# 18 pairs of the first head's maxima between the projections of chunks 11 to 15, and VectorE's rotation steps behind GpSimd's sine

## The reference

```
x:  4 x 2048 x 256, 16 heads of 16
qkv = x @ w_qkv + b_qkv
q, k: from token 679 on, x * cos + rotate_half(x) * sin   (1369 rows of sin and cos)
attn = softmax(q k^T / 4);  out = attn v;  y = out @ w_proj + b_proj
x = layernorm(x + y)
gate, up = fp4(x) @ fp4(w_gate)^T, fp4(x) @ fp4(w_up)^T      (704 wide, blocks of 16)
x = layernorm(x + fp4(silu(gate) * up) @ fp4(w_down)^T)
```

## Time and profile before

| | us |
|---|---|
| median of 3 runs | 3471.18 (3470.55 to 3475.24) |
| profiled execution, its own time | 3468.84 |
| its span, first to last instruction | 3466.9 |
| TensorE busy in it | 3373.9 (97%) |
| VectorE | 3219.7 (93%) |
| ScalarE | 2652.9 (77%) |
| GpSimd | 811.9 (23%) |
| mean granted TensorE clock | 0.983 |

### The profile page before, as it was taken

How to read it: one execution, slowest core, us unless ns; L and a number is a source line. 1 busy time by engine, 2 the same in 40 slices (tenths; PEclk the granted TensorE clock), 3 DMA queues, 4 the chain that set the end, 5 groups by cost and what they waited for, 6 DMA issues and landing times.

```text
span 3466.9 us, 69292 instructions
## 1 busy us (share of the span) xinstructions
PE 3373.9 (97%) x27752; PEld 1516.5 (44%) x27752; DVE 3219.7 (93%) x3525; ACT 2652.9 (77%) x4946; POOL 811.9 (23%) x1045
## 2 busy tenths in 40 slices
PE   8989999999999999999999999999999999999998
PEld 4543333333333333333333333333333346677775
DVE  6778999999999999999999999999999949999997
ACT  5626888888888888888888888888888874444444
POOL 5830210101111001101010110011000016766665
PEclk9978999999999999999999999999999999999999
DMA  4531222222222122211122221122111112211110
GB/s 147 180 121 63 103 91 85 95 84 104 73 85 77 66 79 104 73 55 70 64 82 82 85 89 54 61 83 78 62 61 67 50 40 66 78 50 42 42 36 22
DMA packets 132973, 264.19 MB, mean 76 GB/s; under 512 B 30022, under 2 KB 84518, under 8 KB 114214
## 3 DMA queue, kind: packets, MB, share of 16 engines
q1 hardware_dynamic: 119520, 243.25, 19.9%
q10 hardware_dynamic: 13132, 16.52, 1.5%
HBM read 173.11 MB, written 84.93 MB: 74 GB/s over the span
## 4 chain that ended last, share of the span: by engine, by line
PE 83%; DVE 6%; ACT 4%; POOL 3%; issue 2%; DMA 1%; SPq 0%; ACTq 0%; POOLq 0%; DVEq 0%
PE ps L677 37%; PE ps L730 33%; PE ps L814 6%; PE ps L826 3%; ACT arena L941 2%; PE ps L740 1%; PE ps L717 1%; PE ps L648 1%; ACT arena L916 1%; POOL arena L1273 1%; PE ps L804 1%; DVE arena L1082 1%; POOL arena L1282 0%; DVE arena L1166 0%; DMA arena<-in_xT 0%
## 5 line engine op out<-in xcount | busy, mean ns | idle before, releaser
L1082 DVE TENSOR_REDUCE arena<-ps 128x1 f32<-128x1024 f32 x2048 | 2495.3, 1222 | 61.0 <-PE ps L677 44.9
L941 ACT ACTIVATE arena<-ps 128x512 f32<-128x512 f32 x4096 | 2222.0, 597 | 321.5 <-PE ps L717 236.5
L677 PE MATMUL ps<-kst,qst 48*128 48x512 f32 x4096 | 1518.9, 452 | 14.3 <-DVE arena L1082 12.3
L717 PE MATMUL ps<-qst,kst 51*128 51x512 f32 x4096 | 1497.8, 448 | 0.2
L730 PE MATMUL ps<-arena 128*32 128x256 f32 x16384 | 1309.9, 392 | 16.8 <-ACT arena L916 15.9
L677 PEld LDWEIGHTS ps<-kst,qst 48*128 48x128 f32 x4096 | 613.7, 188 | 871.9 <-DVE arena L1082 700.4
L730 PEld LDWEIGHTS ps<-arena 128*32 128x32 f32 x16384 | 326.3, 108 | 740.3 <-issue 409.0
L717 PEld LDWEIGHTS ps<-qst,kst 51*128 51x128 f32 x4096 | 608.4, 185 | 15.5 <-ACT arena L941 11.4
L1337 POOL TENSOR_TENSOR arena<-arena,ones 128x16 bf16<-128x16 f32 x64 | 14.2, 222 | 2305.1 <-DVE arena L1087 2305.1
L926 ACT ACTIVATE arena<-arena 128x256 f32<-128x256 f32 x64 | 32.7, 511 | 216.5 <-DVE arena L1179 216.5
L814 PE MATMUL ps<-wgT,arena 128*128 128x352 f32 x512 | 193.5, 460 | 0.3 <-DVE v_all L1232 0.3
(11 more groups left out here) (104 smaller groups left out, 2095.3 us busy)
## 6 DMA issues: line engine op xcount, KB each, us to landing
qk_parts<-arena SPq DMA_DIRECT2D x32, 1024.0 KB, 5.6
kst<-qk_parts SPq DMA_DIRECT2D x127, 256.0 KB
qst<-qk_parts SPq DMA_DIRECT2D x127, 256.0 KB
qk_whole<-arena SPq DMA_DIRECT2D x16, 1024.0 KB, 5.0
arena<-qk_whole SPq DMA_DIRECT2D x16, 1024.0 KB, 5.0
kst<-qk_parts SPq DMA_DIRECT2D x127, 128.0 KB
qst<-qk_parts SPq DMA_DIRECT2D x127, 128.0 KB
att<-arena SPq DMA_DIRECT2D x256, 34.0 KB
```

Source lines behind the costliest of these rows:

```text
L677: mm = nc.tensor.matmul(ps[:, i % S_BANKS, :], q[SROW:SROW + STACK, qt * P:(qt + 1) * P], k[SROW:SROW + STACK, kc * CHUNK:(kc + 1) * CHUNK ...
L717: nc.tensor.matmul(ps[:, bank_of_t(g.c, i), :], kst[g.u % 2][first:first + ROWS, kb * P:(kb + 1) * P], qst[g.u % 2][first:first + ROWS, qb ...
L941: nc.scalar.activation(pt[kb % 2][:, qb * CHUNK:(qb + 1) * CHUNK], ps[:, bank_of_t(g.c, i), :], ACT.Exp).then_inc(p_ready, 1)
L1082: nc.vector.tensor_reduce(mx[g.u % 2][:, i // 2, i % 2:i % 2 + 1], ps[:, bank:bank + 2, :].rearrange("p b t -> p (b t)"), AX.X, ALU.max).t ...
```

## The change

- In the first stage TensorE issues 18 pairs of head 0's score tiles between the projections: in chunks 11 to 15, after query-key groups 0, 1 and 3 and after the second value group (in chunk 11 only the last two places). They use banks 6 and 7, one pair at a time: pair k waits for k maxima. VectorE takes the maxima around its cosine and addition.
- VectorE's cosine has lag 1 now and waits for GpSimd's sine of the same chunk. The cosine and the addition of the last chunk come after pairs 9 and 19 of head 1, and SyncE's store of that chunk after the first maxima rows, ahead of `head` 0.
- The first batch is split one step earlier, both pieces of a half in one step (steps 5 and 6), and head 0's `load_s` comes from SyncE in step 6; head 1's `load_s` in step 12 and head 0's `load_t` in step 13.
- Buffers of the arena change places, so that the attention's first buffers lie where chunks 13 and 14 were; GpSimd's constants are written at the start; the bias is added in step 8.

```diff
-FIRST_SPLIT = 4
+FIRST_SPLIT = 3
+EARLY_AT = [(n, slot) for n in range(11, NCH) for slot in (0, 1, 3, 5)][2:]
+EARLY = len(EARLY_AT)
+BIAS_AT, LAST_COS, LAST_ROPE = 8, 9, 19
+def s_bank(g, i):
+    return 6 + i % 2 if g.c * PAIRS + i // 2 < EARLY else i % S_BANKS
...
# SyncE
-                if n.c == FIRST_SPLIT + 2:
+                if n.c == FIRST_SPLIT + 1:
                     store_split(0, 0)
+                    load_whole(0, 1)
                 if n.c == FIRST_SPLIT + 3:
-                    load_whole(0, 1)
-                if n.c == FIRST_SPLIT + 5:
                     store_split(0, 1)
-            run_straight(NCH, [(0, store_parts), (0, split_first)])
-            load_t(0, 0)
-            load_s(0, 1)
-            wait_stores(sp, NCH)
+                    sp.wait_ge(split_out, 16 * PARTS * 2)
+                    load_s(0, 0)
+                if n.c == FIRST_SPLIT + 9:
+                    load_s(0, 1)
+                if n.c == FIRST_SPLIT + 10:
+                    load_t(0, 0)
+            run_straight(NCH - 1, [(0, store_parts), (0, split_first)])
...
             load_maxima(0)
+            store_parts(At(0, NCH - 1))
...
                 if g in JOB_AT:
+                    if g == JOB_AT[0]:
+                        wait_stores(sp, NCH)
                     load_job(JOB_AT.index(g))
...
# TensorE: early_pair(n, m) after each query-key group, early_pair(n, 4 + v) after each value group
+            def early_pair(n, slot):
+                if (n.c, slot) in EARLY_AT:
+                    k = EARLY_AT.index((n.c, slot))
+                    for i in range(2):
+                        s_tile(At(0, k // PAIRS), 2 * (k % PAIRS) + i)
...
# s_tile
+                if i % 2 == 0 and k == 0:
+                    pe.wait_ge(prep, 6)
+                    pe.wait_ge(bias_done, 1)
+                elif i % 2 == 0 and k < EARLY:
+                    pe.wait_ge(s_done, k)
+                elif i % 2 == 0 and k >= EARLY + 2:
+                    pe.wait_ge(s_done, k - 1)
...
# VectorE
             def times_cos(n):
                 x = qx[n.c % 3]
                 dve.wait_ge(rot_ready, n.times(2, 2))
+                dve.wait_ge(rotsin, n.times(1, 1))
...
-            run_straight(NCH, [(1, rope), (0, times_cos), (0, later_weights)])
+            run_straight(NCH, [(0, lambda n: early_pairs(n, (0, 1))), (1, beside(times_cos)),
+                               (0, lambda n: early_pairs(n, (3,))), (1, beside(rope)),
+                               (0, lambda n: early_pairs(n, (5,))), (0, later_weights)])
...
+                    if g.c * PAIRS + i >= EARLY:
+                        pair_of_maxima(g, i)
+                    if g.c == 1 and i == LAST_COS:
+                        times_cos(At(0, NCH - 1))
+                    if g.c == 1 and i == LAST_ROPE:
+                        rope(At(0, NCH - 1))
...
# GpSimd
             def split_first(n):
                 for u in range(2):
-                    piece = n.c - FIRST_SPLIT - 3 * u - 2
-                    if 0 <= piece < PIECES:
-                        split(u, piece)
+                    if n.c == FIRST_SPLIT + 2 + u:
+                        for piece in range(PIECES):
+                            split(u, piece)
```

More of the change, by code:

```diff
@@ L292, in layer_kernel @@
         pt = [take(N) for _ in range(2)]
+        at_r = [take(CT * P, "p (c t) -> p c t", c=CT) for _ in range(4)]
+        jobs = [take(2 * CHUNK) for _ in range(JOB_BUFS)]
         vs = [take(KT * 32, "p (t d) -> p t d", t=KT) for _ in range(2)]
@@ L650, in project @@
                     mm.then_inc(qk_psum, 1)
+                    early_pair(n, m)
                 if n.static(0):
@@ L660, in project @@
                     mm.then_inc(v_psum, 1)
[L662 to L666 removed]
+                    early_pair(n, 4 + v)
+            def early_pair(n, slot):
[3 more added lines that the diff above has]
+                        s_tile(At(0, k // PAIRS), 2 * (k % PAIRS) + i)
             def s_tile(g, i):
                 pair = i // 2
+                k = g.c * PAIRS + pair
                 if i == 0:
                     pe.wait_ge(s_in[g.u % 2], g.quad(128, 64 * (g.u // 2 + 1)))
[L673 to L674 removed]
+                if i % 2 == 0 and k == 0:
[5 more added lines that the diff above has]
+                    pe.wait_ge(s_done, k - 1)
                 qt, kc = i // CHUNKS, i % CHUNKS
                 q, k = qst[g.u % 2], kst[g.u % 2]
[L677 removed]
+                mm = nc.tensor.matmul(ps[:, s_bank(g, i), :], q[SROW:SROW + STACK, qt * P:(qt + 1) * P],
                                       k[SROW:SROW + STACK, kc * CHUNK:(kc + 1) * CHUNK], start=True, stop=True)
@@ L680, in s_tile @@
                     mm.then_inc(s_psum, 1)
+            run_straight(NCH, [(0, project), (2, weights)])
+            pe.wait_ge(qk_out, 4 * NCH)
             def t_bank_free(place):
@@ L779, in head @@
                                 xT_tile(At(0, 0))
-            for i in range(TILES_S):
+            for i in range(2 * EARLY, TILES_S):
                 s_tile(At(0, 0), i)
@@ L956, in _ @@
             act.wait_ge(b_const, 3)
+            for p in (1, 2):
+                act.wait_ge(parts_out[p], 16 * (NCH // 3))
             each_head(head)
@@ new lines, in early_pairs, with beside @@
+            def early_pairs(n, slots):
+                for slot in slots:
+                    if (n.c, slot) in EARLY_AT:
+                        k = EARLY_AT.index((n.c, slot))
+                        pair_of_maxima(At(0, k // PAIRS), k % PAIRS)
+            def beside(fn):
+                return lambda n: fn(n) if n.c < NCH - 1 else None
+            run_straight(NCH, [(0, lambda n: early_pairs(n, (0, 1))), (1, beside(times_cos)),
+                               (0, lambda n: early_pairs(n, (3,))), (1, beside(rope)),
+                               (0, lambda n: early_pairs(n, (5,))), (0, later_weights)])
@@ L1258, in _ @@
             nc.gpsimd.memset(wu_n[LEFT:P, 5, :], 0.0).then_inc(w_pad, 1)
+            pool.wait_ge(w_pad, 1)
+            nc.gpsimd.memset(ones[:, :], 1.0)
+            for s in range(2):
+                mm = nc.gpsimd.memset(kst[s][0:MROWS, :].bitcast(F32), 1.0)
+            mm.then_inc(b_const, 1)
+            pool.wait_ge(b_const, 1)
             def round_weights(w):
@@ L1295, in _ @@
             run_straight(NCH, [(0, times_sin), (0, split_first), (0, later_weights)])
-            wait_stores(pool, NCH)
-            for s in range(2):
-                mm = nc.gpsimd.memset(kst[s][0:MROWS, :].bitcast(F32), 1.0)
-            mm.then_inc(b_const, 1)
-            pool.wait_ge(b_const, 1)
-            nc.gpsimd.memset(ones[:, :], 1.0)
+            pool.wait_ge(qr_done, NCH - 1)
             for p in range(2):
```

38 lines of the change are left out of this document (16 added, 22 removed).

## The result

| | us |
|---|---|
| kernel before, median of the same chip's runs | 3471.18 (3463.79 to 3475.24) |
| changed kernel, median of 5 runs | 3488.05 (3485.82 to 3499.74) |
| ratio of paired runs | 1.0065 [1.0052, 1.0077] |
| profiled execution before / after | 3468.84 / 3494.57 |
| its span | 3466.9 / 3492.4 |

By the ratio the change makes the kernel slower by 0.65%, 22.5 us: 3493.7 on the time shown before. (The medians alone differ by 16.9; the ratio pairs each run with a run of the kernel before.) The forecast said 3483, 12 us slower, with a range up to 3491. The sign and the late mechanism are those of the forecast; the size is not, and the part of it that went wrong lies in the first stage.

What follows compares the result with a forecast made beforehand. It took TensorE's chain of waits and clock as the bound. Dense work 16.4 us earlier but head 2's rows late gave +1.6, plus 11.2 of low clock: +12.8 on 3468.84, 3481.6, stated as 3483; range 3466 to 3491.

Steps and rivals of the forecast that it cites:

- D: Start of the dense work after the first head's maxima and ten pairs of the second; 268.43 before, predicted 252.0.
- The store behind pair 19: SyncE's store of chunk 15 waits for the addition behind head 1's pair 19, D + 24.3; head 2's row loads queue behind.
- the wait at tile 44: In head 0's dense work TensorE waits 16.0 us for head 2's rows, in at D + 55.3; bounds 3.6 and 20.
- the clock's term: After the wait for head 2's rows TensorE runs 26.1 us at 1.2 GHz, costing 11.2 us; bounds nearly nothing and 22.
- Rival 2: Clock doesn't fall after the last chunk, so D = 251.2 and the sum is +5.5 us, 3476.7; chance 0.2 in all.
- rival 3: Head 2's rows arrive in time, TensorE waits 3.6 us at most; -10.8 us, 3460; chance 0.09.
- Rival 1: Clock comes back soon after the stall for head 2's rows; +3.3 us, 3474.5, no change; chance 0.15.
- the gain ahead of it: First head's maxima end at 240.3 instead of 256.7, so dense work starts 16.4 us earlier; bounds 13 to 20.
- a stall that did not occur: Chunk 12: pairs wait for all maxima before them, predicted to cost TensorE 0.9 us once.
- The store of chunk 7: Issued at 143.6, slowed by head 0's row loads, lands near 153.3; chunk 11 starts 5.0 us later, at 158.2.
- 18 pairs x 0.585 = 10.5: Chunks 11 to 15: the early pairs add 10.5 us to TensorE, 0.585 us each at the full clock.
- rival 4: More goes wrong in the first stage, or the low clock lasts 40 us; +20 us, 3491; chance 0.11.

Runs made afterwards that it cites:

- e1_rows_first: Changed kernel with SyncE storing chunk 15 behind head 0's row loads instead of ahead of them; 3463.95 us, ratio 0.9982.
- e7_rotation_early: Changed kernel with the last chunk's cosine and addition behind pairs 0 and 1 of head 1, not 9 and 19; 3464.82 us, ratio 0.9990.
- e6_filler_fit: Changed kernel with 21 unused filler matmuls on TensorE ahead of head 0's tile 44, in place of the wait; 3482.43 us, ratio 1.0030.
- e2_rows_later: Changed kernel with head 0's rows loaded behind the store of chunk 8, and 16 pairs from chunk 12 on; 3485.96 us, ratio 1.0038.
- e5_no_pairs: Changed kernel without its 18 early pairs, all else kept; 3500.5 us, ratio 1.0081.
- e13_eight_engines: Changed kernel with each head's rows loaded by twelve transfers of 8 rows instead of four of 16 and 32; 3485.08 us, ratio 1.0046.
- e8_warm: e1_rows_first with one unused 128x256 filler matmul behind each of 22 pairs between the last chunk and the dense work; 3489.74 us, ratio 1.0049.
- e9_rows_halved: e1_rows_first with head 0's row loads in two halves, behind the stores of chunks 8 and 9, and 14 pairs; 3455.55 us, ratio 0.9953.
- e10_warm_start: e1_rows_first with three filler matmuls in each of two start gaps and a 128x128 filler behind each pair; 3475.49 us, ratio 1.0014.
- e3_both: Changed kernel with the moves of e1_rows_first and e2_rows_later together; 3462.82 us, ratio 0.9984.
- e12_halved_no_pairs: e9_rows_halved without any pair of the first head between the chunks; 3464.19 us, ratio 0.9981.
- e14_eight_and_order: e1_rows_first with each head's rows loaded by twelve transfers of 8 rows; 3464.46 us, ratio 0.9987.

## Why the prediction was right in sign and wrong in size

Step by step, predicted and measured in the profile after:

| step | predicted | measured |
|---|---|---|
| addition of chunk 7 ends | 143.6 | 144.2 |
| store of chunk 7 lets ScalarE go on | 153.3 | 157.7 |
| chunk 11 starts | 158.2 | 165.4 |
| a pair on TensorE | 0.585 | 0.86 |
| first head's maxima end | 240.3 | 250.9 |
| D | 252.0 | 262.6 |
| addition of chunk 15 ends | D + 24.3 | D + 24.2 |
| tile 44's rows are in | D + 55.3 | D + 55.9 |
| TensorE waits there | 16.0 | 18.1 |
| low clock after it costs | 11.2 | 10.2 |

**What held.** The store behind pair 19, the loads queued behind it, the wait at tile 44 and the clock behind it are as written, within about 2 us each. (The wait is 2.1 longer since TensorE reached tile 44 at D + 37.8 and not D + 39.3, and the rows came at D + 55.9.) The runs show each by itself: e1_rows_first and e7_rotation_early take the wait away and end 23 to 24 us lower; e6_filler_fit takes the clock's part away alone. That the clock's term came within 1.0 is in part luck: it took the length of one low stretch, 26.1 us, for another. Behind the same wait the low clock lasted 23.8 us here, but 15.2 in e2_rows_later, 30.5 in e5_no_pairs and 34.6 in e13_eight_engines, which at 0.43 is 6.5 to 14.9 us. Rival 2 (the clock stays up after the last chunk) fell: it was low from 236.5 on. So did rival 3, the rows in time: they were 18 late. Rival 1, the clock soon back, fell as well: after the wait it took 23.8 us of work, and in e8_warm TensorE was busy in 49.80 of 51.00 us and then in 25.00 of 25.00 at half clock. The Trainium skill (TensorE: Matmul & The Clock Gate, "What's actually happening") says that activity releases the throttle. These stretches don't agree with it; nearer to it is chunk 10, where the clock was back 5.8 us after TensorE went on (158.96 to 164.8, busy throughout).

**What failed: the gain ahead of it, 16.4 us predicted and 5.8 measured.** Two terms of the sum were too small, by 7.2 and 5.0; less the 0.9 of a stall that did not occur that is 11.3, of which 10.6 show.

- *The store of chunk 7, "5.0 us later"*: 12.2. It was issued 0.6 late and landed 13.5 us after its issue, where I had added 9.7; by that TensorE went on at 158.96 and not 154.7, which is 4.3 of it. The other 2.9 are the clock, which I had not counted: it fell in that wait of 8.56, and chunk 10's value group took 6.59 us and not 3.6. The bound that I gave, 8 us, was for another mishap. e2_rows_later and e9_rows_halved show the cause: with the row loads elsewhere or in halves, this wait is 0.9 or 1.0. It was not a want of bandwidth in all: from 154 to 158 us, with the store still out, the DMA share was 0.18 at 70 GB/s, the work of some 3 of 16 engines.
- *"18 pairs x 0.585 = 10.5"*: 18 x 0.86 = 15.5. I took 1.17/2 from pairs in a row. Between two groups of 128x512 a pair takes 0.66 by starts, and the four matmuls around it take 1.91 where four of sixteen in 7.03 are 1.76 without a change of shape; the value groups pay likewise. e5_no_pairs shows the sum of it, a chunk of 10.32 us without pairs and of 13.75 with four.

By steps, the 13.0 us between 3481.6 and the profiled 3494.57 are: D later by 10.6, the rows by 0.6, the clock -1.0, and 2.8 behind head 2, nearly all of it in the last stage.

**The chances.** "Slower" at 0.58 was the right lean. The range ended at 3491 since rival 4, more going wrong in the first stage, had +20 at most, counted from before instead of on top of the forecast's own wait and clock. A later D goes through the sum at full size: the wait at tile 44 moves with it.

**What stays open.** The low clock after D, with the same mix of work, lasted 26.1 us before, 21.7 in the changed kernel, 10.6 in e1_rows_first, 17.6 in e7_rotation_early, 23.7 in e9_rows_halved, 28.2 in e5_no_pairs and 29.5 in e8_warm; at 0.43 that is 8 us between the shortest and the longest. I found nothing in the traces that orders these. It need not be a matter of the kernel: e1_rows_first's ten runs go from 3460.76 us at a mean granted clock of 0.989 to 3474.45 at 0.985, and one of them was profiled. Nor is it settled what holds the row loads at 50 to 110 GB/s: the number of engines is a part, shown by e13_eight_engines, and not all of it.

## What to carry to other kernels

When a step is moved later, go to the in-order queue that waits for it, list what stands behind that wait, and ask where the first of those is needed; here one swap in SyncE's list was worth 24 us (29 by the ratios), and with the loads of one head in two halves the same change went from 0.65% slower to 0.5% faster. Price an inserted instruction by its neighbours of another shape, in place, and not by its rate in a row. Give every new wait on TensorE two prices, its own and the low clock's behind it: from 100 us on, half clock came with every wait of 3.8 us or more in these traces.

## What the runs showed of the hardware that I had not expected

- A busy TensorE did not get its clock back: 78.5 us at 1.2 GHz in e8_warm, of which it idled under 2, and 40.9 of 40.9 busy in e10_warm_start. In the latter the clock fell at 238.4 with TensorE busy for 37.91 of the 38.30 us ahead of it, and no wait over 0.4. The fillers multiply by an identity; whether other data would do otherwise wasn't tried.
- A wait of 1.61 us at the full clock was followed by half clock in five kernels (e2_rows_later and e3_both 7 us, e10_warm_start 14, e12_halved_no_pairs and e14_eight_and_order 17), and by none in e1_rows_first and e13_eight_engines.
- The share of 0.13 under the last row loads is the work of 2 of 16 engines, and 0.48 with loads of 8 rows that of 8. The Trainium skill (DMA: Bandwidth & Descriptors, on why a DMA increments its semaphore by 16 and not by 1) says that a transfer uses the largest number of engines up to 16 that divides the slowest dimension of both sides, here 2, and 8 for the loads of 8 rows; the traces agree. More engines did not give more bandwidth in proportion.
- Four row loads (768 KB) delay what is issued behind them: a store of 1 MB took 13.5 us to land (line's median 5.0 before) and, in e2_rows_later, a load of x^T from another queue 14.0. In halves they cost TensorE 1.0 us, and no load of x^T was waited for.
- A filler matmul of 128x512 takes 0.87 us at the full clock, 18.29 us for 21, and is recorded as two; a score tile of the same width takes one record of 0.39 to 0.50.
